# Attention and FFN on one core: silu through tanh, norms on ScalarE, weight splits behind the first norm, PE spun at the start, a token-major last tile

## What is computed

```python
x = x + LN(attn(LN(x)))
x = x + LN(ffn(LN(x)))

# attn, weights Wq1, Wk1 (256,128), Wq2, Wk2 (128,512), Wv (256,512), Wo (512,256)
q = silu(x @ Wq1 @ Wq2)
v = x @ Wv
f = sigmoid(x @ Wk1 @ Wk2)
a = sigmoid(f)                      # exp(log_sigmoid(f))
h[t] = a[t] * h[t-1] + (1 - a[t]) * v[t]    # a scan along the 512 tokens
out = q * h
out = out * rsqrt(mean(out * out) + 1e-6) * norm_w
return out @ Wo

# ffn, 6 blocks; LN_g with gain and bias behind the first five
x = gelu(x @ W1.T + b1) @ W2.T + b2 + x ;  x = LN_g(x)
```

## Time and profile before

| | before |
|---|---|
| median of 3 executions | 681.07 us (678.48 to 681.57) |
| the profiled execution | 681.17 us, its span 679.4 us |
| PE busy | 638.5 us, 94% of the span |
| DVE busy | 488.8 us, 72% |
| ACT busy | 379.9 us, 56% |
| POOL busy | 277.9 us, 41% |
| HBM | 28 GB/s over the span |

### The profile page before, as it was taken

How to read it: one execution, slowest core, us unless ns; L and a number is a source line. 1 busy time by engine, 2 the same in 40 slices (tenths; PEclk the granted TensorE clock), 3 DMA queues, 4 the chain that set the end, 5 groups by cost and what they waited for, 6 DMA issues and landing times.

```text
span 679.4 us, 8587 instructions
## 1 busy us (share of the span) xinstructions
PE 638.5 (94%) x2944; PEld 528.0 (78%) x2944; DVE 488.8 (72%) x829; ACT 379.9 (56%) x611; POOL 277.9 (41%) x232
## 2 busy tenths in 40 slices
PE   1979899989999999999999999999999999999994
PEld 0768678868788788887888887888878888888883
DVE  6899998797985866577666766676687666764554
ACT  3566384746665755556655566555575555554440
POOL 4576653366842633216521247123272321222223
PEclk9979899999999999999999999999999999999997
DMA  7111000000210200001200003000010000000001
GB/s 273 62 34 61 0 1 1 0 1 1 89 36 0 94 32 0 1 0 40 86 0 1 1 6 119 0 1 1 0 63 0 1 1 0 1 1 32 32 15 48
DMA packets 8684, 19.35 MB, mean 28 GB/s; under 512 B 1600, under 2 KB 4672, under 8 KB 8640
## 3 DMA queue, kind: packets, MB, share of 16 engines
q1 hardware_dynamic: 8064, 18.27, 7.8%
q10 hardware_dynamic: 576, 0.52, 0.2%
HBM read 16.69 MB, written 2.10 MB: 28 GB/s over the span
## 4 chain that ended last, share of the span: by engine, by line
PE 79%; DVE 13%; issue 4%; POOL 2%; ACT 1%; POOLq 0%; DVEq 0%; ACTq 0%
PE BK L393 39%; PE BK L614 36%; DVE R L356 4%; PE BK L482 2%; DVE SB L464 1%; DVE ST L342 1%; DVE OL L473 1%; DVE R L509 1%; DVE HL L606 1%; PE BK L534 1%; DVE R L632 1%; DVE P L531 1%; PE BK L367 1%; DVE KB L461 0%; DVE AB L459 0%
## 5 line engine op out<-in xcount | busy, mean ns | idle before, releaser
L600 ACT ACTIVATE HH<-BK,B 128x512 fp32r<-128x512 f32 x192 | 132.5, 690 | 220.3 <-PE BK L393 216.9
L606 DVE TENSOR_TENSOR HL<-BK,HH 128x512 fp32r<-128x512 f32 x192 | 131.3, 686 | 137.1 <-ACT BK L603 136.5
L393 PE MATMUL BK<-XH,WL 128*128 128x512 f32 x432 | 173.9, 403 | 3.7 <-DVE XL L380 3.7
L393 PE MATMUL BK<-XH,WH 128*128 128x512 f32 x432 | 170.0, 393 | 0.0
L393 PE MATMUL BK<-XL,WH 128*128 128x512 f32 x432 | 169.2, 392 | 0.0
L614 PE MATMUL BK<-HH,WL 128*128 128x512 f32 x384 | 151.2, 394 | 0.0
L614 PE MATMUL BK<-HL,WH 128*128 128x512 f32 x384 | 149.7, 390 | 0.0
L614 PE MATMUL BK<-HH,WH 128*128 128x512 f32 x384 | 149.4, 389 | 0.0
L603 ACT ACTIVATE BK<-BK,B 128x512 f32<-128x512 f32 x192 | 125.4, 653 | 0.0
L393 PEld LDWEIGHTS BK<-XH,WL 128*128 128x128 f32 x432 | 81.8, 189 | 20.8 <-DVE XL L380 5.0
L393 PEld LDWEIGHTS BK<-XH,WH 128*128 128x128 f32 x432 | 81.6, 189 | 17.8
(11 more groups left out here) (86 smaller groups left out, 761.8 us busy)
## 6 DMA issues: line engine op xcount, KB each, us to landing
STG<-in_w SPq DMA_DIRECT2D x24, 512.0 KB, 3.5
out<-R SPq DMA_DIRECT2D x16, 128.0 KB, 1.9
X<-in_x SPq DMA_DIRECT2D x3, 512.0 KB, 7.3
R<-in_wv SPq DMA_DIRECT2D x1, 512.0 KB, 5.2
STG<-in_wo SPq DMA_DIRECT2D x1, 512.0 KB, 5.9
X<-in_x ACTq DMA_DIRECT2D x2, 128.0 KB, 3.0
X<-in_x SPq DMA_DIRECT2D x2, 128.0 KB, 2.8
R<-in_wq SPq DMA_DIRECT2D x1, 256.0 KB, 4.2
```

What stands on the lines that cost most here:

```text
L393: r = e.matmul(dst, s, m, start=first and i == 0, stop=last and i == len(todo) - 1)
L600: lambda e, ev=ev, hs=hs, bias=bias: e.activation(HH[:, hs, :], bank_of[ev][:, :], ACT.Gelu, bias=bias),
L606: lambda e, ev=ev, hs=hs: e.tensor_tensor(HL[:, hs, :], bank_of[ev][:, :], HH[:, hs, :].bitcast(f32), ALU.subtract), ("hlo", n, j))
```

## The change

- Silu goes. In its place, for each zq, ACT takes tanh(z/2) from PSUM into QB, and DVE forms (tanh + 1) * z with z from PSUM: twice silu. The factor is taken up in the RMS epsilon. The wait of `o` is now on its own m.
- `a` (L459) moves from DVE to ACT, as Identity with scale 0.5 and a bias tile of 0.5.
- All norms of attention (l1, l2, l3) move from DVE to ACT, as Identity with scale and bias tiles. POOL forms the bias: `ng` (minus the mean) and `nb` (times rs), two more small operations for each norm.
- RI (L506) and `pev` (L509) go: l2's statistics and norm read PA in PSUM, and the RMS factor enters l2's epsilon (`ve` becomes a sum of variance and MS). norm_w is negated on POOL, which takes up the sign of `pev`. The next tile's first proj waits for l2's norms.
- The remainders of the first weights wait until tile 0's first norm is issued and done.
- PE runs 17 matmuls of 512 columns on a tile of ones at the start.
- The warm-up activation is Gelu.
- The last tile (n = 23) accumulates by token: its residual (with bias, by ACT) enters four PSUM banks by a matmul with the identity before mm2, mm2 is issued with the hidden features as the stationary side (12 matmuls of 256 columns for each j), and the last two j are issued chunk by chunk. Statistics, centring (ACT), the final multiply-add (DVE) and the store then go chunk by chunk. Two ring banks are claimed for it.
- LASTS gets new durations, so the order on every engine is planned anew.

```diff
+SPIN = 17
+TAIL = 2
...
-LASTS = {"sync": 0.1, "scalar": 0.55, "vector": 0.6, "gpsimd": 1.2, "tensor": 1.29,
...
+LASTS = {"sync": 0.1, "scalar": 0.6, "vector": 0.68, "gpsimd": 1.31, "tensor": 1.36,
...
+        op("gpsimd", -98, [], lambda e: e.memset(OH[:, 0, :].bitcast(f32), 1.0), ("idle_in",))
+
+        def spin(e):
+            for i in range(SPIN):
+                r = e.matmul(PA[1][:, :], OH[:, 0, 0:128], OH[:, 0, :], start=True, stop=True)
+            return r
+        op("tensor", -100, [("idle_in",)], spin, ("spin",))
...
-                  [("ldw_" + w,)], lo_engine="vector" if w in ("q1", "k1") else "gpsimd")
...
+                  [("ldw_" + w,)], lo_waits=[("l1_nm", 0, c) for c in range(4)], lo_engine="vector" if w in ("q1", "k1") else "gpsimd")
...
+            op("gpsimd", key + gap * 4 + 0.7, [(name + "_rs", t), (name + "_ng", t)],
+               lambda e: e.tensor_tensor(NBS[:, t, :], NM[:, t, :], RS[:, t, :], ALU.mult), (name + "_nb", t))
...
-                op("vector", key + gap * c, [(name + "_rs", t), *extra],
-                   lambda e, c=c: e.tensor_scalar(dst[:, c, :], src[:, c, :], MV[:, t, c, 0:1],
-                                                  RS[:, t, c:c + 1], ALU.subtract, ALU.mult),
+                op("scalar", key + gap * c, [(name + "_nb", t), (name + "_rs", t), *extra],
+                   lambda e, c=c: e.activation(dst[:, c, :], src(c), ACT.Identity, bias=NBS[:, t, c:c + 1],
+                                               scale=RS[:, t, c:c + 1]),
...
-                op("vector", A + 0.9 + 0.8 * m, [ev, *used],
-                   lambda e, m=m, ev=ev: e.tensor_copy(QB[:, m, :], bank_of[ev][:, :]), ("zc", t, m))
...
+                op("scalar", A + 0.9 + 0.8 * m, [ev, *used],
+                   lambda e, m=m, ev=ev: e.activation(QB[:, m, :], bank_of[ev][:, :], ACT.Tanh, scale=0.5), ("tq", t, m))
+                op("vector", A + 1.6 + 0.8 * m, [("tq", t, m), ev],
+                   lambda e, m=m, ev=ev: e.scalar_tensor_tensor(QB[:, m, :], QB[:, m, :], 1.0, bank_of[ev][:, :],
+                                                                ALU.add, ALU.mult), ("q", t, m))
...
-                op("vector", M + 2.4, [("t2", t, m), *before("scan")],
-                   lambda e, ab=ab, kb=kb: e.tensor_scalar(ab, kb, 0.5, 0.5, ALU.mult, ALU.add), ("a", t, m))
+                op("scalar", M + 2.4, [("t2", t, m), ("half",), *before("scan")],
+                   lambda e, ab=ab, kb=kb: e.activation(ab, kb, ACT.Identity, scale=0.5, bias=HALF[:, :]), ("a", t, m))
...
-            op("gpsimd", Z + 0.5, [("ms", t), ("mhalf",)],
-               lambda e, t=t: e.tensor_tensor(RI[:, t, :], MS[:, t, :], MH[:, 0:4], ALU.pow), ("ri", t))
...
+            stats(Z + 1, "l2", t, p_of, lambda c, t=t: [("proj", t, m) for m in range(4)], 0.4)
+            norm(Z + 4.5, "l2", t, R[:, t], p_of, 0.3, [("turn", "l1", t, k) for k in range(2)])
...
+            def put(e):
+                for c in range(4):
+                    for k in range(2):
+                        r = e.matmul(END[c][:, 128 * k:128 * k + 128], feat(t, k)[:, c, :], ID[:, :],
+                                     start=(k == 0), stop=False, skip_group_check=True)
+                return r
+            op("tensor", K, [("res", 0), ("res", 1), *(("z_nm", n - 2, c) for c in range(4)),
+                             ("claim", RING - 2), ("claim", RING - 1)], put, ("inj", n))
...
+                op("vector", K + 0.4, [("end", c)], lambda e, c=c: e.bn_stats(ST[:, t, c, :], END[c][:, 0:256]), ("z_st", n, c))
...
+                op("vector", K + 2.0, [("z_ct", c), ("z_rs", n, c), ("inj", n)],
+                   lambda e, c=c, half=half: e.scalar_tensor_tensor(R[:, t, c, :], half, RS[:, t, c:c + 1], X[:, t, c, :],
+                                                                    ALU.mult, ALU.add), ("fin0", t, c))
+                load(K + 3, out[t][:, c, :], R[:, t, c, :], ("stored", t, c), [("fin0", t, c)])
...
+                def by_token(e, chunks=range(4), b=b, j=j, hs=hs):
+                    a = 2048 + 256 * j
+                    wh, wl = WH[:, b % 2, a:a + 256], WL[:, b % 2, a:a + 256]
+                    for c in chunks:
+                        hh, hl = (h[:, hs, c * 128:(c + 1) * 128] for h in (HH, HL))
+                        for i, (h, w) in enumerate(((hh, wl), (hh, wh), (hl, wh))):
+                            r = e.matmul(END[c][:, 0:256], h, w, start=False, stop=(j == 7 and i == 2),
+                                         skip_group_check=True)
+                    return r
```

More of the change, by code:

```diff
@@ L270, in sandwich @@
         op("gpsimd", -99, [], lambda e: e.memset(QU[:, :], 0.25), ("quarter",))
-        op("scalar", -98, [("one",)], lambda e: e.activation(WARM[:, :], ONE[:, :], ACT.Silu), ("warm",))
+        op("gpsimd", -98.9, [], lambda e: e.memset(HALF[:, :], 0.5), ("half",))
+        op("gpsimd", -4, [("ldnw",)], lambda e: e.tensor_scalar(NW[:, :], NW[:, :], -1.0, 1.0, ALU.mult, ALU.mult), ("nw",))
+        op("gpsimd", -98, [], lambda e: e.memset(OH[:, 0, :].bitcast(f32), 1.0), ("idle_in",))
[4 more added lines that the diff above has]
+        op("tensor", -100, [("idle_in",)], spin, ("spin",))
+        op("scalar", -98, [("one",)], lambda e: e.activation(WARM[:, :], ONE[:, :], ACT.Gelu), ("warm",))
         def split(key, src, hi, lo, name, ready, hi_waits=(), lo_waits=(), lo_engine="gpsimd"):
@@ L345, in stats @@
                    lambda e, c=c: e.bn_aggr(MV[:, t, c, :], ST[:, t, c, :]), (name + "_mv", t, c))
-            op("gpsimd", key + gap * 4 + 0.5, [(name + "_mv", t, 3)],
-               lambda e: e.tensor_scalar(VE[:, t, :], MV[:, t, :, 1], EPS_LN, 1.0, ALU.add, ALU.mult),
-               (name + "_ve", t))
+            every = [(name + "_mv", t, c) for c in range(4)]
+            if name == "l2":
+                op("gpsimd", key + gap * 4 + 0.5, [*every, ("ms", t)],
+                   lambda e: e.tensor_tensor(VE[:, t, :], MV[:, t, :, 1], MS[:, t, :], ALU.add), (name + "_ve", t))
+            else:
+                op("gpsimd", key + gap * 4 + 0.5, every,
+                   lambda e: e.tensor_scalar(VE[:, t, :], MV[:, t, :, 1], EPS_LN, 1.0, ALU.add, ALU.mult),
+                   (name + "_ve", t))
+            op("gpsimd", key + gap * 4 + 0.55, every,
+               lambda e: e.tensor_scalar(NM[:, t, :], MV[:, t, :, 0], -1.0, 1.0, ALU.mult, ALU.mult), (name + "_ng", t))
             op("gpsimd", key + gap * 4 + 0.6, [(name + "_ve", t), ("mhalf",)],
@@ L485, in sandwich @@
                 op("tensor", M + 8.8, [("olo", t, m), ("ohi", t, m), ("wo_lo",)]
-                   + ([("after", ("proj", t, m - 1))] if m else [("pev", t - 1, 3)] if t else []), proj, ("proj", t, m))
+                   + ([("after", ("proj", t, m - 1))] if m else [("l2_nm", t - 1, c) for c in range(4)] if t else []), proj, ("proj", t, m))
             for m in range(1, 4):
@@ L573, in layer_norm, with inject @@
                    ("xlo", name, t, k))
+        END = [ACC[0][0], ACC[0][1], BK[RING - 2], BK[RING - 1]]
+        ends = []
+        def inject(K, n, t, b):
+            for k in range(2):
+                op("scalar", K - 12 + 0.7 * k, [("xlo", f"f{b - 1}", t, k), ("bias",), ("ldb2",)],
+                   lambda e, k=k: e.activation(feat(t, k), feat(t, k), ACT.Identity,
+                                               bias=BS[:, 2 * b + k:2 * b + k + 1]), ("res", k))
+            def put(e):
+                for c in range(4):
+                    for k in range(2):
+                        r = e.matmul(END[c][:, 128 * k:128 * k + 128], feat(t, k)[:, c, :], ID[:, :],
[3 more added lines that the diff above has]
+                             ("claim", RING - 2), ("claim", RING - 1)], put, ("inj", n))
@@ L638, in sandwich, with token @@
                 continue
-            def token(c, acc=acc, last=last):
-                return BK[c][:, 0:256] if last else ACC[acc][c // 2][:, (c % 2) * 256:(c % 2) * 256 + 256]
+            def token(c, acc=acc):
+                return ACC[acc][c // 2][:, (c % 2) * 256:(c % 2) * 256 + 256]
             for c in range(4):
@@ L649, in tr @@
                     return m
-                S = 1.3 if not last else 0.9
-                K = E + 2 + S * c
-                op("tensor", K, [("y", n, k, c // 2) if last else ("y", n, k) for k in range(2)], tr, ("ft", n, c))
-                seen = ("ft", n, c if last else c | 1)
+                K = E + 2 + 1.3 * c
+                op("tensor", K, [("y", n, k) for k in range(2)], tr, ("ft", n, c))
+                seen = ("ft", n, c | 1)
                 op("vector", K + 0.5, [seen], lambda e, t=t, c=c, token=token: e.bn_stats(ST[:, t, c, :], token(c)),
```

101 lines of the change are left out of this document (65 added, 36 removed), and 3 rows, old and new, of the table LASTS.

## The result

The kernel after takes 664.25 us (median; 663.48 to 665.20) against 681.32 for the kernel before beside it: a ratio of 0.976 (0.973 to 0.979), 17 us less. The profiled execution took 664.7, its span 662.9; before it was 681.2 and 679.4, so the two spans differ by 16.5 us, and that is what has to be found.

A forecast was written before the change was run, and what follows sets the result against it. Attention was taken as bound by DVE, with PE waiting; 681.2 less start 3.7, spin 1.7, middle 10 and end 4.0 gave 661.8, so 662 us, range 656 to 668 (chance 0.60), 652 to 673 for 8 in 10.

The forecast's parts named there:

- The sum: Whole kernel: 681.2 - 3.7 - 1.7 - 10 - 4.0 = 661.8 us, so 662.
- The start: Before the first transposes at 14.18 us: first norm on ACT brings them to 10.5, gain 3.7 us (3.0 to 4.8).
- The terms of the norm: First four norms on ACT: about 0.5 us each in a row, after splits until 7.8, ending at 9.9.
- The spin: PE's 17 warm-up matmuls: keep the fast clock for first transposes and u, gain 1.7 us, bounds 0 and 3.4.
- The middle: 14.18 to 200 us, attention: of about 19 us of PE's waits for DVE and clock falls, 10 won (3 to 17).
- The 52 us: Attention from 14.18 to 200 us: DVE's net relief, 63 - 11 = 52 us less of 163.
- the change doesn't do what it says: Rival: table reloads remain in the mixed part, some twenty switches of 1.28 us, 675 us; chance 0.02.
- What is late next is ACT: Attention after the change: ACT at 143 us of 186, needing 23 us a tile where PE needs 22 to 23.
- Steady: From 200 to 668.5 us: PE dense, 459 of 468.5 us, so the change adds nothing there.
- every order is new: Sign of a wrong forecast: the stretch from 200 us on no longer full; no size given.
- norms block ACT: Rival: norms at the head of ACT's queue wait for POOL, middle loses 16 us more, 688 us; chance 0.03.
- The end: Last tile and tail: 10.9 us behind the last matmul become 5.2, identity matmuls cost 1.7; net 4.0 (2 to 5.5).
- Token-major mm2 costs nothing: Last tile: 12 matmuls of 256 columns at 0.114 us take 1.37 us against 1.36 before.

The follow-up runs named there:

- the repaired start: Kernel after with v's high part issued behind the four first norms on ACT and 28 spin matmuls instead of 17; 661.52 us (0.972).
- The two kernels with exchanged durations: Kernel before planned with the changed kernel's durations, 701.25 us (1.029); kernel after planned with the old durations, 689.75 us (1.013).
- the kernel after once more: Kernel after with mm1 of the last tile's groups above 3 also waiting for the identity matmuls, same order on every engine; 663.76 us (0.975).

## Why the prediction was right, step by step

**The sum** gave 661.8, measured were 664.7 in the profiled execution and 664.25 in the median. The three places (DVE in the middle, the norm at the start, the end behind the last matmul) were right, and putting the norms or `a` back on DVE cost 10 and 8 us. The sizes of all terms were off, and partly made up for each other: 1.5 too much at the start, 3.6 too much in the middle with the spin, 0.8 too much at the end, and 3.1 not foreseen from 200 us on. That the sum came within 3 us is to that extent luck.

**The start, 3.7 against 2.2.** The terms of the norm held: ACT took four in a row in 2.06 us (in the repaired start) where 2.0 was forecast. But v's split stands whole between the third and the fourth norm (1.04 us where I allowed half), and ACT waited for data before it could end the first splits, which put them at 8.7 and not at 7.8. The weights' landing isn't the change's: in the profiles of the eight kernels with this very order of ACT at the start, the transposes began at 11.02 to 12.32. So the gain is 1.9 to 3.2 us against the one 14.18 of before, where my bounds were 3.0 to 4.8. The term was mis-sized, by a row I had, and one I took for fixed (the splits until 7.8).

**The spin, 1.7 against 0.4.** "The spin's warmth may be lost before it is used" is what happened. The bounds 0 and 3.4 held, and the middle of them was the wrong choice: with the spin done at 7, the early end of my 7 to 9 (it was 7.1), and the transposes at 10.5 by my own sum, the gap would be 3.5 us. The gap that the earlier trace rows shows losing the clock was no longer: by its row PE was idle for 6.20 - 3.01 = 3.2 us, which I had put at 3.5. The repaired start shows the fast clock through the transposes and u, so the upper end was there to be had.

**The middle, 10 (and the spin) against 8.1.** ACT's load was forecast at 143 us of 186 and is 143.3 of 188; POOL's 110 is 117. DVE's 111 is 136.5, and three things stand in between. The 52 us were counts times mean durations, and over the whole kernel the sum of DVE's durations did fall by 51 (534.7 to 484.1); but successive instructions overlap in it, and busy time, which counts such time once, fell by 38 (488.8 to 450.7). The first four norms, 6.3 us, lay in front of 14.18 and were never part of the 162.7. And the stretch holds more of the FFN than before (894 matmuls, not 847). One group also grew that the change doesn't touch: 40 multiply-adds of the FFN's norm went from 748 to 880 ns each, 5.3 us.

```profile
L586 DVE SCALAR_TENSOR_TENSOR R<-R,LG,MB 128x512 f32<-128x512 f32 x40 | 33.6, 880 | 0.0
L487 ACT ACTIVATE AB<-KB,HALF 128x512 f32<-128x512 f32 x16 | 11.7, 729 | 0.1
L380 ACT ACTIVATE R<-X,NBS,RS 128x256 f32<-128x256 f32 x32 | 17.3, 590 | 0.0
L288 ACT ACT_TABLE_LOAD x1 | 1.3, 1283 | 2.6 <-issue 2.6
```

The rows before that fence's last say the sizes of single operations were right: `a` 0.73 on ACT (0.72 forecast), a norm 0.59. The last says that one table load is left of four: the rival "the change doesn't do what it says" fell. For that rival I had set the Trainium skill's list of tables (ScalarE: Activation LUTs, section Table sets), by which tanh and Gelu would reload; here they alternate with one load, and the measurement decides.

The 10 was a share of the waits for DVE, and the waits that went are those behind 100 us. Up to there they stayed, and 3.1 of the 8.1 us are less time at the half clock. How much of that is the clock's own chance can be seen in the two executions of after, where it differs by 1.3 us (5.0 and 3.7).

"What is late next is ACT" is not confirmed. PE waited for ACT's norm at the start, and once more for 1.1 us where the next tile's first proj waits for l2's norms, and `a` taken off ACT made the kernel slower. What is late next by the rows is proj at DVE's remainder (7.6 us), in the longest case behind POOL's queue, and that POOL is the cause was only argued: with x1 taken off POOL the time went to other waits, which another order alone does too. In 20 to 50 us ACT has 8.3 to 10.0 of every 10 us and POOL 9.4 to 9.6; the losses left sit on an order of nearly full engines, and no single move that I tried gives them back.

**Steady, 0 against 3.1.** I called this stretch dense and left it. From 200 to 600 us PE lost 9.4 before and 6.5 after. Of the 2.9 us 2.8 can be named. Before, the small matmul of the FFN's norm (L534, 16 columns) waited four times for its partial sums from DVE, and after has no such wait there:

```profile
PE BK L534 <- DVE P L531: 2.8, 4, 0.7
```

The two kernels with exchanged durations lose 20.0 and 14.5 us in this stretch, which holds next to nothing but FFN work, so it is the order that moves it. The prediction knew that "every order is new" and gave it no price. By these two kernels, 20 and 25 us hang on durations that fit the code, which is more than the whole gain; the change's code under the old durations is slower than the kernel before. That was the largest thing missing from the prediction: a rival of its own, on the slower side, in place of the one where norms block ACT. The trace of before holds one order, so it had no row for this price. What stays open is the other side of it: no run here planned the old code with further sets of durations, so it isn't known whether a luckier order alone would have given the kernel before a part of the 17 us.

**The end, 4.0 against 3.2.** Chunks 0.72 us apart (0.68 forecast), two powers queued on POOL, 5.6 us from the last matmul's start to the end: this part came as forecast. The identity matmuls start at 637.73 and the next matmul at 639.43, 1.7 us, as the value taken:

```profile
637.73 1.95 PE L610 MATMUL BK<-ID,R 128*128 128x128 f32 x16
```

There are eight in the code and 16 in the trace: each is done as two, at 0.106 us. The step that failed is "Token-major mm2 costs nothing": the 96 matmuls come 0.120 us apart where 0.114 was taken, and with the switches between groups they cost 0.8 us. No wait stands at the claim of the ring banks.

**The parts don't add up.** Undone one at a time, the norms, `a`, Silu and the tail cost 10, 8, 6.4 and 2.4 us, 27 together, where the whole change gave 17. Part of each of the first three is the order and the clock that came with it: they were planned with durations that had been picked for the changed kernel. So each number is what the part is worth in this kernel with these durations, and not its share of the gain; how the 17 us divide between the moved work and the order isn't shown. The tail's part alone is free of this (3.2 us by the traces, the orders in front of it being the same).

## What to carry to other kernels

Weigh a stretch by what PE loses against its pace, and price a start by every instruction that stands on the engine between data and first use, the split that lands in between included; a warm-up pays only if it reaches to within the gap that the trace shows to be harmless (here 2.2 us was, 4.8 wasn't, and 3.1 was in one execution of three). In a kernel whose order comes from a planner, the durations given to it are a part of the change as large as the work that it moves: run the old code with the new durations, and the new with the old, before a gain is put down to the code. Differences below what a small change of durations alone makes (2.9 us here, from one such change) say nothing on the part that was edited, unless the traces show the same order up to the edit.

## What the runs showed of the hardware

**One gap of 3.1 us, three outcomes.** The proj that ends PE's gap at 64 us, in the kernel without a spin and in the kernel after once more (in the kernel after it is the row at 67.20 above):

```profile
67.33 0.39 PE L509 MATMUL BK<-WH,OL 128*128 128x256 f32 x1 [3.08 <-DVE OL L500]
```

```profile
66.95 0.55 PE L510 MATMUL BK<-WH,OL 128*128 128x256 f32 x1 [3.10 <-DVE OL L501]
```

The idle times are 3.08, 3.10 and, in after, 3.08 us. PE and POOL have the same order in all three. In the first the clock didn't fall and the matmul took 0.39 us; in the second it fell for 3.4 us, in after for 6.8 (the window from 66.0 to 73.1, clock 0.52). The same 135 matmuls, from the proj at 61 us on, took 29.4, 30.3 and 31.4 us. So such a fall costs 0.8 or 1.9 us here, less than the 1.7 and 3.4 that half pace would make if nothing else were waited for, and 2 us between two profiles don't prove a cause.

**The first weights land at no fixed time.** ACT's first split began at 5.32 us in the kernel after once more, 5.37 without the spin, 6.00 with `a` on DVE, and 7.15 with the old last tile, all with the same loads in front of it, and the transposes follow it, at 11.17, 11.02, 11.40 and 12.22.

**A norm on DVE waits out a whole instruction of POOL; on ACT it doesn't.** Four norms of 256 columns took 1.38 us with POOL quiet and 5.30 beside its tensor_tensors of 1.3 us, in one and the same execution: 0.41 us each, or 1.35 to 1.48. On ACT none of the 32 took more than 0.60.
